# Joined and paired lower-part matmuls in a scan with an MLP, and a new order of the waits around them

## The reference

```python
x = x + _L0_conv_ref(_gn(x), ...)
x = x + _L1_conv_ref(_gn(x), ...)
# _L0_conv_ref, on 7 x 7 windows, 49 tokens one after another:
w = _ln(w, ln1_w, ln1_b)
xB = w @ Bm
h = xb + h @ A          # the scan's step, xb a token of xB
w = h @ Cm              # over all steps
y = _ln(xr, ln2_w, ln2_b)
y = jax.nn.gelu(y @ W1 + b1, approximate=False) @ W2 + b2
return xr + y
```

## Time and profile before

| | |
|---|---|
| time, median of 3 runs | 4492.68 us (4488.22 to 4493.79) |
| profiled execution, its time | 4493.39 us |
| its span | 4491.6 us |
| PE busy | 4286.1 us (95%), 52040 matmuls |
| PE weight loads busy | 3664.5 us (82%) |
| DVE busy | 3938.4 us (88%) |
| ACT busy | 2479.7 us (55%) |
| POOL busy | 2584.4 us (58%) |

### The profile page before, as it was taken

How to read it: one execution, slowest core, us unless ns; L and a number is a source line. 1 busy time by engine, 2 the same in 40 slices (tenths; PEclk the granted TensorE clock), 3 DMA queues, 4 the chain that set the end, 5 groups by cost and what they waited for, 6 DMA issues and landing times. The chain is left out here.

```text
span 4491.6 us, 141866 instructions
## 1 busy us (share of the span) xinstructions
PE 4286.1 (95%) x52040; PEld 3664.5 (82%) x52040; DVE 3938.4 (88%) x8102; ACT 2479.7 (55%) x4852; POOL 2584.4 (58%) x2092
## 2 busy tenths in 40 slices
PE   0699999999999999999996999999999999999999
PEld 0588888888888888888885888888888888888887
DVE  8688888888888888888884999999899899999998
ACT  0244444444444444444442777777777777777776
POOL 0255554445545545555444777777767767777766
PEclk9999999999999999999997999999999999999999
DMA  8011111111111111111111222222222222222222
GB/s 362 23 40 40 40 40 37 38 39 39 39 39 39 39 40 40 40 40 40 37 39 41 78 77 76 76 78 76 77 75 75 76 77 75 77 76 76 79 76 64
DMA packets 390776, 284.66 MB, mean 63 GB/s; under 512 B 148159, under 2 KB 389188, under 8 KB 389700
## 3 DMA queue, kind: packets, MB, share of 16 engines
q1 hardware_dynamic: 387612, 281.57, 21.6%
q10 hardware_dynamic: 3112, 2.39, 0.2%
HBM read 119.00 MB, written 87.31 MB: 46 GB/s over the span
## 5 line engine op out<-in xcount | busy, mean ns | idle before, releaser
L904 POOL TENSOR_TENSOR L<-L,mx 128x588 f32<-128x588 f32 x512 | 600.2, 1172 | 596.1 <-DVE mx L1127 596.1
L608 PE MATMUL ps_o<-w,g_hi 128*128 128x384 f32 x2352 | 710.9, 365 | 5.9 <-DVE g_lo L548 4.1
L418 ACT ACTIVATE gF<-ps_g,b1f 128x512 f32<-128x512 f32 x588 | 406.2, 691 | 393.8 <-PE ps_g L639 391.3
L898 POOL TENSOR_TENSOR E<-E,ri 128x588 f32<-128x588 f32 x512 | 600.2, 1172 | 0.8 <-DVE ri L1133 0.8
L608 PE MATMUL ps_o<-w,g_lo 128*128 128x192 f32 x2352 | 534.3, 254 | 0.0
L447 POOL TENSOR_TENSOR res<-xt,b2b 128x768 f32<-128x768 f32 x98 | 181.0, 1847 | 590.9 <-DVE x L496 590.9
L1189 PE MATMUL ps_s<-Kp,Q 32*64 32x98 f32 x12288 | 493.6, 258 | 21.9 <-issue 18.8
L404 ACT ACTIVATE h_hi<-ps_h,hbias 128x512 fp32r<-128x512 f32 x196 | 123.2, 680 | 703.2 <-PE ps_h L623 703.2
L1011 ACT ACTIVATE o_hi<-ps_v,vb 128x98 fp32r<-128x98 f32 (+1 forms) x1024 | 290.2, 335 | 300.6 <-PE ps_v L1302 292.8
L608 PEld LDWEIGHTS ps_o<-w,g_hi 128*128 128x128 f32 x2352 | 429.3, 189 | 27.1 <-issue 25.1
L608 PEld LDWEIGHTS ps_o<-w,g_lo 128*128 128x128 f32 x2352 | 443.7, 191 | 0.0
(11 more groups left out here) (220 smaller groups left out, 12446.9 us busy)
## 6 DMA issues: line engine op xcount, KB each, us to landing
xs<-in_x SPq DMA_DIRECT2D x8, 4704.0 KB, 22.7
xt<-in_x SPq DMA_DIRECT2D x98, 384.0 KB, 3.4
xb<-x_cells SPq DMA_DIRECT2D x128, 294.0 KB
Vx<-V SPq DMA_DIRECT2D x512, 73.5 KB
out<-yo SPq DMA_DIRECT2D x128, 294.0 KB
x_cells<-x SPq DMA_DIRECT2D x780, 48.0 KB
Kp<-K SPq DMA_DIRECT2D x256, 98.0 KB, 2.0
Kp<-K SPq DMA_DIRECT2D x256, 49.0 KB, 2.2
```

Source lines behind the costliest of these rows:

```text
L418: act.activation(gF[f % 4][:, :], ps_g[:, f % 2, :], ACT.Gelu, bias=b1f[:, f:f + 1]).then_inc(s_gelu, 1)
L608: last = pe.matmul(dst, g[:, f, P * k:P * (k + 1)], w, start=(f == 0 and i == 0), stop=(f == FT - 1 and i == 1))
L898: pool.tensor_tensor(e, e, ri[p][:, :].unsqueeze(2).to_broadcast([P, HEADS, T]), ALU.mult)\
L904: pool.tensor_tensor(l, l, mx[p][:, :].unsqueeze(2).to_broadcast([P, HEADS, T]), ALU.subtract).then_inc(s_sub, 1)
```

## The change

Six edits, all in the MLP stage but for a few set-up operations:

1. **Joined lower parts.** In the scan the fifth product of `Bm` and that of `A` become one: `W_AB_b_lo` holds the lower b weights of Bm in rows 0 to 63 and of A in rows 64 to 127, and a new tile `xh_b` holds the upper b data of xn and of h in the same rows. 18 matmuls instead of 20. ScalarE makes two more copies (64 x 512) for it.
2. **Blocks in pairs as row tiles.** In the first MLP product the fifth matmul of a block has 64 rows only. Two blocks stand together: eight full matmuls, then one of 64 rows in rows 0 to 63 for the first block and one in rows 64 to 127 for the second, which reads a copy `y_b` of the same data (one more ScalarE copy). Blocks 2 and 3 now go to the banks of `ps_r`, so the product with Cm waits for their GELU.
3. **Second product in three parts.** `second_layer(0)` runs blocks 0 and 1, then 2 and 3, then 4 and 5, each behind a wait of its own.
4. **Upper and lower signals apart.** Each of the two upper copies gives a signal of its own, and VectorE waits for them one by one.
5. **Order on VectorE.** `xn` is normalised before `g_lo` of blocks 0 and 1; `g_lo` of blocks 4 and 5 moves behind the statistics of the second layer norm.
6. **GELU order on ScalarE.** Two GELUs, then their two upper copies.

The group norm stays on VectorE as before.

```diff
-                        for t in range(2):
+                        for t in range(1 if parts in (W_A, W_B) else 2):
...
+                    dve.wait_ge(s_wh, 1)
+                    for full, parts, rows in ((fold_B, W_B, slice(0, CB)), (raw_A, W_A, slice(CB, P))):
+                        dve.tensor_tensor(W_AB_b_lo[rows, :], full[rows, 1, :], parts.parts[2][rows, :], ALU.subtract)
...
+            def ps_f(f):
+                return (ps_r if f // 2 == 1 else ps_g)[:, f % 2, :]
...
-                def upper_parts(hi, full):
-                    act.activation(hi[:, 0, :], full[:, 0, :], ACT.Copy)
-                    return act.activation(hi[0:CB, 1, :], full[0:CB, 1, :], ACT.Copy)
+                def upper_parts(hi, full, ready):
+                    act.activation(hi[:, 0, :], full[:, 0, :], ACT.Copy).then_inc(ready, 1)
+                    act.activation(hi[0:CB, 1, :], full[0:CB, 1, :], ACT.Copy).then_inc(ready, 1)
...
-                            last = act.activation(h_hi[d][0:rows, k, :], ps_h[0:rows, k, :], ACT.Identity,
-                                                  bias=hbias[0:rows, k:k + 1])
-                        last.then_inc(s_hh, 1)
+                            act.activation(h_hi[d][0:rows, k, :], ps_h[0:rows, k, :], ACT.Identity,
+                                           bias=hbias[0:rows, k:k + 1]).then_inc(s_hh, 1)
                     if there(n):
                         act.wait_ge(s_t2, n + 1)
-                        upper_parts(y_hi, ps_g).then_inc(s_yh, 1)
+                        upper_parts(y_hi, ps_g, s_yh)
+                        act.wait_ge(s_yh, 2 * n + 2)
+                        act.activation(y_b[CB:P, :], y_hi[0:CB, 1, :], ACT.Copy).then_inc(s_yb, 1)
                     if there(n):
-                        for f in range(FT):
-                            act.wait_ge(s_w1, FT * n + f + 1)
-                            if f == 0:
-                                upto(act, s_w2, n)
-                            elif f >= 4:
-                                act.wait_ge(s_gld, len(LO_DVE) * n + LO_DVE.index(f - 4) + 1)
-                            act.activation(gF[f % 4][:, :], ps_g[:, f % 2, :], ACT.Gelu,
-                                           bias=b1f[:, f:f + 1]).then_inc(s_gelu, 1)
-                            for g in range(max(f - 1, 0), f + (f == FT - 1)):
+                        for f in range(0, FT, 2):
+                            for g in (f, f + 1):
+                                act.wait_ge(s_w1, FT * n + g + 1)
+                                if g == 0:
+                                    upto(act, s_w2, n)
+                                elif g >= 4:
+                                    act.wait_ge(s_gld, len(LO_DVE) * n + LO_DVE.index(g - 4) + 1)
+                                act.activation(gF[g % 4][:, :], ps_f(g), ACT.Gelu,
+                                               bias=b1f[:, g:g + 1]).then_inc(s_gelu, 1)
+                            for g in (f, f + 1):
                                 act.wait_ge(s_gelu, FT * n + g + 1)
                                 act.activation(g_hi[:, g, :], gF[g % 4][:, :], ACT.Copy).then_inc(s_gh, 1)
...
-                        upper_parts(xn_hi[c], ps_h).then_inc(s_xh, 1)
+                        upper_parts(xn_hi[c], ps_h, s_xh)
+                        act.wait_ge(s_xh, 2 * n + 6)
+                        act.activation(xh_b[c][0:CB, :], xn_hi[c][0:CB, 1, :], ACT.Copy).then_inc(s_xs, 1)
+                    if there(n + 1):
+                        act.wait_ge(s_hh, 2 * n + 4)
+                        act.activation(xh_b[1 - c][CB:P, :], h_hi[1 - c][0:CB, 1, :], ACT.Copy).then_inc(s_hs, 1)
...
-                def lower_parts(hi, lo, full, bias=None):
+                def lower_parts(hi, lo, full, upper, count, ready, bias=None):
                     for k, rows, dst in ((0, P, lo[:, :]), (1, CB, hi[CB:P, 1, :])):
                         src, up = full[0:rows, k, :], hi[0:rows, k, :]
+                        dve.wait_ge(upper, count + k - 1)
                         if bias is None:
-                            last = dve.tensor_tensor(dst, src, up, ALU.subtract)
+                            dve.tensor_tensor(dst, src, up, ALU.subtract).then_inc(ready, 1)
                         else:
-                            last = dve.scalar_tensor_tensor(out=dst, in0=src, scalar=bias[0:rows, k:k + 1], in1=up,
-                                                            op0=ALU.add, op1=ALU.subtract)
-                    return last
+                            dve.scalar_tensor_tensor(out=dst, in0=src, scalar=bias[0:rows, k:k + 1], in1=up,
+                                                     op0=ALU.add, op1=ALU.subtract).then_inc(ready, 1)
...
-                        dve.wait_ge(s_hh, n + 2)
-                        lower_parts(h_hi[1 - c], h_lo[1 - c], ps_h, hbias).then_inc(s_hl, 1)
+                        lower_parts(h_hi[1 - c], h_lo[1 - c], ps_h, s_hh, 2 * n + 4, s_hl, hbias)
                     if there(n):
-                        dve.wait_ge(s_yh, n + 1)
-                        lower_parts(y_hi, y_lo, ps_g).then_inc(s_yl, 1)
+                        lower_parts(y_hi, y_lo, ps_g, s_yh, 2 * n + 2, s_yl)
...
-                    if there(n):
-                        for f in LO_DVE[:2]:
-                            dve.wait_ge(s_gh, FT * n + f + 1)
-                            dve.tensor_tensor(g_lo[:, f, :], gF[f % 4][:, :], g_hi[:, f, :], ALU.subtract)\
-                                .then_inc(s_gld, 1)
-                    if there(n + 2):
                         dve.wait_ge(s_rs1, n + 3)
...
-                        for f in LO_DVE[2:]:
+                        for f in LO_DVE[:2]:
...
+                    if there(n):
+                        for f in LO_DVE[2:]:
+                            dve.wait_ge(s_gh, FT * n + f + 1)
+                            dve.tensor_tensor(g_lo[:, f, :], gF[f % 4][:, :], g_hi[:, f, :], ALU.subtract)\
+                                .then_inc(s_gld, 1)
                     if there(n + 2):
-                        dve.wait_ge(s_xh, n + 3)
-                        lower_parts(xn_hi[c], xn_lo[c], ps_h).then_inc(s_xl, 1)
+                        lower_parts(xn_hi[c], xn_lo[c], ps_h, s_xh, 2 * n + 6, s_xl)
...
-                def second_layer(half):
+                def second_layer(half, blocks=range(FT)):
                     for k in (2 * half, 2 * half + 1):
-                        for f in range(FT):
+                        for f in blocks:
...
-                        pe.wait_ge(s_xl, n + 2)
-                        upto(pe, s_hl, n)
+                        pe.wait_ge(s_xl, 2 * n + 4)
+                        pe.wait_ge(s_xs, n + 2)
+                        upto(pe, s_hl, 2 * n)
+                        upto(pe, s_hs, n)
                         for m, rows in enumerate((P, CB)):
                             cols = slice(P * m, P * m + rows)
-                            terms = (*W_B.terms(xn_hi[d], xn_lo[d], cols), *W_A.terms(h_hi[d], h_lo[d], cols))
+                            terms = (*W_B.terms(xn_hi[d], xn_lo[d], cols)[0:4], *W_A.terms(h_hi[d], h_lo[d], cols)[0:4],
+                                     (W_AB_b_lo[:, cols], xh_b[d][:, :]))
...
-                        pe.wait_ge(s_yl, n + 1)
-                        for f in range(FT):
-                            if f >= 2:
-                                pe.wait_ge(s_gelu, FT * n + f - 1)
-                            terms = W_1.terms(y_hi, y_lo, slice(P * f, P * (f + 1)))
-                            for k, (w, v) in enumerate(terms):
-                                last = pe.matmul(ps_g[:, f % 2, :], w, v, start=(k == 0), stop=(k == len(terms) - 1))
-                            last.then_inc(s_w1, 1)
+                        pe.wait_ge(s_yl, 2 * n + 2)
+                        for f in range(0, FT, 2):
+                            if f == 2:
+                                pe.wait_ge(s_rsum, n + 1)
+                            if f == 4:
+                                pe.wait_ge(s_gelu, FT * n + 2)
+                            for g in (f, f + 1):
+                                terms = W_1.terms(y_hi, y_lo, slice(P * g, P * (g + 1)))[0:4]
+                                for k, (w, v) in enumerate(terms):
+                                    pe.matmul(ps_f(g), w, v, start=(k == 0), stop=False)
+                            if f == 0:
+                                pe.wait_ge(s_yb, n + 1)
+                            w = W_1.parts[3]
+                            pe.matmul(ps_f(f), w[0:CB, P * f:P * (f + 1)], y_hi[0:CB, 1, :],
+                                      start=False, stop=True).then_inc(s_w1, 1)
+                            pe.matmul(ps_f(f + 1), w[CB:P, P * (f + 1):P * (f + 2)], y_b[CB:P, :],
+                                      start=False, stop=True).then_inc(s_w1, 1)
                     if there(n + 1):
                         d = 1 - c
```

(18 more changed lines are left out.)

## The result

The changed kernel takes 4514.2 us, median of 5 runs (4513.1 to 4517.26), beside 4493.8 of the kernel before in the same comparison: ratio 1.0046, 95% interval 1.0035 to 1.0057, 20 us slower. The forecast's sum was 4498, which would be no difference, with a range of 4448 to 4540 and 0.40 for slower, 0.34 for faster. The time lies in the range, but outside the 4488 to 4508 that the case of the sum was given: it lies between the sum and the rival with another wait (4531).

The account below looks back on a forecast made before the run. It took the DMA queue (SP's stores and xt load) with VectorE as the bound. After the change, 8.50 + 9.73 + 0.33 + 4.36 = 22.92 us a step against 22.83, +8.5 us, less 4 outside the loop: 4498, range 4448 to 4540.

Parts of the forecast that it names:

- the case of the sum: The prediction's own summed step of 22.92 us, giving 4498 us; chance 0.38 for 4488 to 4508.
- the rival with another wait: GpSimd's last sum again holds up VectorE's group norm subtraction: +0.35 us a step, 4531 us; chance 0.17.
- the collision: GpSimd's last sum running into VectorE's group norm subtraction: 1.38 us against 0.96; forecast as gone after the change.
- (b): First MLP product and product with Cm on TensorE: 9.13 us becomes 9.73, as each row-tile pair costs +0.20.
- (c): From the last Cm matmul to the second layer norm's statistics: 0.33 us.
- (d): VectorE from the second layer norm's statistics through g_lo 4 and 5 to the lower parts of xn: 4.36 us.
- (a): From the lower parts of xn to the first MLP product, TensorE and VectorE equally long: 8.50 us.
- free by a hair: Group norm subtraction starts 6.17 us after the variance; GpSimd lets go at 6.14, a margin of 0.03 us.
- the third of the rivals: Another wait: GpSimd's last sum holds up the group norm subtraction, +0.35 us a step, 4531 us; chance 0.17.
- What bounds the kernel before: SP's stores and xt load, 16.27 us, plus VectorE's 6.56 us were read as the 22.83 us step.
- the rival of 4450: Tile shape changes cost little, so the DMA queue bounds at 22.41 us a step: 4450 us; chance 0.15.
- The joined scan brings nothing of its own: In the scan, 0.46 us less on TensorE gains nothing, as VectorE stands beside it with the same length.

Follow-up runs that it names:

- a_no_last_sum: Changed kernel with GpSimd's last sum of a step cut to four elements: 4498 us, a step of 22.91 us.
- b_joined_more: Kernel before plus the joined scan, GpSimd's two sums moved behind the next group norm, and the xt load ahead of the stores: 4447 us.
- both v kernels: Changed kernel with full fifth matmuls, GpSimd's sums later and xt load ahead: 4443 us; the same with g_lo 4 and 5 ahead of the statistics: 4437 us.
- a_full5: Changed kernel with the fifth matmuls of a pair full again (128 rows) instead of row tiles: 4464 us.
- a_scan10: Changed kernel with the joined lower parts undone, 20 scan matmuls a step instead of 18, ScalarE's copies kept: 4542 us.
- b_joined: Kernel before plus the joined lower parts in the scan alone (18 matmuls, two more ScalarE copies): 4480 us.
- b_joined_load: Kernel before plus the joined scan and the xt load ahead of the stores, GpSimd's sums where they were: 4481 us.
- a_glo_first: Changed kernel with g_lo of blocks 4 and 5 back ahead of the second layer norm's statistics on VectorE: 4544 us.

## Why the prediction was right and where it failed

The time fell into the range, and the sum holds for the kernel without the collision: a_no_last_sum took 22.91 us a step and 4498 us, for the 22.92 and 4498 of the sum. But the range was wide and held both signs, and the case that the sum was given ended at 4508. That 4514 still lies in the range is so because the range was drawn to hold the rival with another wait.

**(b) held.** The three prices from attention, +0.09, +0.12 and +0.11 twice, gave 0.20 a pair; 0.18 was measured, and undoing the row tiles gave back 50 us. (3503.75 - 3503.49 against 0.18 is 0.08, not 0.09, and 3505.71 - 3505.52 is 0.19: the 0.17 is right from the last of the four tiles there. Neither moves the sum by more than 0.01 a pair.) The Trainium skill, "TensorEngine Tiling (Array Packing)", section "Theoretical Speedup", promises up to 2x for 64 rows. The trace agrees in that the two tiles start together (both at 1006.63). But the one matmul saved of ten is 0.23 us, and the changes of shape around it cost 0.41, so the pair got slower.

**(c) and (d) held**, to 0.05 us.

**(a) was mis-sized by 0.21 us.** The step that failed is the one on L505, the subtraction: "free by a hair". It took GpSimd's length after the variance from before, 6.14 us to where it lets go. But the change puts `g_lo` 4 and 5, with two SBUF inputs, right beside `rsb`: 1.41 us in every kernel with this order, instead of the 1.01 that it takes in every kernel where they stand elsewhere. GpSimd's sum then ended 22.92 - 16.31 = 6.61 us after the variance instead of 6.29 (6.55 instead of 6.16 on average over the steps), and the margin of 0.03 us was gone. This is the third of the rivals, in its place, and with a size of 0.31 us a step (1.27 on average for 0.96) where it had 0.35. What it says against itself, that GpSimd's order is unchanged, is true and missed the point: VectorE's order had changed beside it. And only 16 of these 29 us lay on the path (a_no_last_sum), since TensorE stood beside it with nearly the same length. The Trainium skill, "SBUF — State Buffer", section "Terms", has VectorE and GpSimd share a port pair that one instruction holds to its end. The runs agree, in both directions: 1.41 for 1.01 us on GpSimd, 2.11 for 0.96 us on VectorE.

**What bounds the kernel before was wrong**, though the sum didn't rest on it. The wait for `xt` was read as the loop that sets the step. It only filled time that VectorE would have spent in the collision, or waiting for the scan: the load could go and the collision with it, and the time stayed (4492). Whether the queue would be the bound at 22.41 us, the floor on which the rival of 4450 rested, stays open: b_joined_more and both v kernels go below it (22.35, 22.36 and 22.29), but they issue the load ahead of the stores. With the queue as it was, no kernel got below 22.55 (a_full5), and there a part of the wait for `xt` had come back.

**"The joined scan brings nothing of its own" was wrong**, by the prediction's own terms too: VectorE needs 8.44 us there, and TensorE would need 8.90 without it. With 8.90 in place of 8.44 the sum is 23.38 us a step, and a_scan10, without the joined scan, took 23.37, which is 0.46 more than a_no_last_sum. It brings 28 us in the changed kernel, where the collision hides a part of it, and 12 alone in the kernel before.

The sum of all: row tiles +50, joined scan -28, each measured by undoing it in the changed kernel, and the place of `g_lo` 4 and 5 -30 likewise. These don't add up to the +20. Each stands in a step whose loops nearly tie, so they need not; how the rest splits isn't shown. What the separate signals, the parts of the second product, the order of the GELUs and the earlier `xn` bring in the loop wasn't tried alone; the tail shows the parts at work, and the 5 us outside the loop are not split further.

## What to carry to other kernels

Price a change of tile shape on TensorE as a fixed cost on both sides of the tiles, and put many tile matmuls behind one change: one matmul saved of ten doesn't pay for it. A wait in the profile is not a bound until something that hangs on it moves: look whether the instruction behind the wait ends later than it would without. When an instruction with two SBUF inputs is moved on VectorE, look at what GpSimd does beside its old place and its new one, and add up GpSimd's chain as a loop of its own.

## What had not been expected of the hardware

The same subtraction on VectorE took 0.96, 1.28 to 1.36, and 2.11 to 2.13 us, by how early it started beside GpSimd's sum. However early that was, it ended at the same time after the variance, on average over the steps: at 6.96 to 6.98 us in the four kernels with the full sum in its old place and `rsb` at 1.01 us (before, b_joined, b_joined_load, a_glo_first), and at 7.36 to 7.39 in the three with `rsb` at 1.41 (after, a_full5, a_scan10). GpSimd's rsqrt of 128 x 4 elements was lengthened by 0.40 us by two subtractions of VectorE's beside it. And moving these two from ahead of a layer norm's statistics to behind them changed the time by -30 us or +6 us, depending on where GpSimd's sums stood.
